# Two tile shapes on TensorE: v beside q and k in 32x32 tiles, router logits straight onto token partitions

## The chip, the core and the metric

The kernel runs on one core of a Trainium2 chip. A core has five engines that work at the same time and wait for each other by semaphores: TensorE (PE, matrix products, with its weight loads shown apart as PEld), VectorE (DVE), ScalarE (ACT), GpSimd (POOL) and SyncE (SP, which here only issues DMAs). The metric is the device time of one launch in microseconds (us).

## What is computed

The input is x, eight images of 64 channels and 96x96 pixels, in float32. A block of two halves is computed, and cut to what matters it is this:

```python
x = x + conv_ref(ln_c(x))             # LN over channels; windowed attention twice (shift 0 and 2)
t = to_tokens(x)
t = t + ffn(ln_t(t))                  # LN over channels; 8 experts, the best 2 of a token
# attention, on each half of the channels (c = 32): 8 heads of 4 channels, windows of 4x4 pixels
q, k, v = split(einsum('oi,bihw->bohw', qkv_w, xh), 3)
lepe = depthwise_conv3x3(v)
attn = softmax(einsum('nhqc,nhkc->nhqk', q * scale, k) + bias)
out  = einsum('nhqk,nhkc->nhqc', attn, v) + lepe
# ffn, on each token
probs = softmax(x @ router_w + router_b)          # 8 logits
top_p, top_i = top_k(probs, 2); top_p = top_p / sum(top_p)
out = sum over the 2 of top_p * (x @ expert_w[e] + expert_b[e])
```

## The kernel before

The images are cut into 192 strips of four pixel rows (384 pixels), a strip into three units of eight windows; two strips make a tile of the second half (96 tiles). The 128 partitions hold four groups of 32 channels: two halves of the channels, plain and rolled.

One function, `pipeline`, runs the same `slot` on every engine. A slot is one unit further along; `LAG` says how many slots after a unit's start each stage works on it, so in one slot each engine does pieces of many stages, in the order in which its `slot` is written. A tile is six slots. 72 slots (12 tiles, one image) are written out before a loop, 72 are the body of a loop of six turns, the rest stands behind it, so PE's program is a long list without repeats inside a turn. No scheduler moves anything: the order on each engine is that of the code. SP and POOL issue their DMAs in that order too, and a wait holds up all that is behind it on the same engine.

PE's stages per tile, with the line that issues them: 6 `score` (L622, 32 products each in 32x32 tiles), 6 `product` (L707, 32 each, 128x32 tiles: contraction over 128 partitions, 32 output partitions), 2 row sums of the softmax (L713, `ones`, four 128x32 tiles), 2 `value` (L647, v, one 128x128 tile), 2 `query_key` (L660 q and L661 k, four 32x32 tiles each), 3 pieces of `conv` (L687, 128x64), 4 `experts` (L607, 128x64), `centre` (L721), `variance` (L638), `tile_sum` (L727) and `tile_variance` (L732), each one 128x128 tile; `router` (L738, logits with the experts on 16 partitions), `logits` (L671, three transposes that put tokens on the partitions), `turn_gates` (L630, a transpose) and `expert_bias` (L746, three products). All is float32; in the trace every float32 product of PE is two weight loads and two matmul records, and a transpose is one of each.

The eight PSUM banks are `bank_s` (two, scores), `bank_o` (bank 2, attention output), `bank_d` (bank 3, row sums), `bank_p` (banks 4 and 5, shared by q, k, v, the two norms, the router and the gates), `bank_c` (6, conv) and `bank_f` (7, experts). ACT takes most things out of PSUM: v (L792), q twice (L810), k (L819), the logits with their bias (L842), and it puts the bias of the next scores into `bank_s` (L802). DVE takes the transposed logits (L989) and works out the gates. POOL spreads k and v into `kx` and `vx` by 8 and 16 DMAs a strip.

## Time and profile before

| | |
|---|---|
| median of three runs | 3484.97 us (3475.89 to 3493.27) |
| the profiled execution, its own time | 3467.97 us |
| its span, first to last instruction | 3466.1 us |
| busy: PE | 3080.1 us (89%) |
| busy: POOL | 2501.0 us (72%) |
| busy: DVE | 2229.3 us (64%) |
| busy: ACT | 1620.3 us (47%) |
| mean granted TensorE clock | 0.943 of full speed |

PE's matmuls are pipelined, and the trace models their ends: a record lasts longer than PE needs before it can go on. What a group costs is therefore read from the start of the group to the start of the next one, not from its length. Where a row of the trace ends in square brackets, the engine was idle before it for that many us, and the name behind the arrow is what ended the idle time; `issue` means that nothing was waited for that the profile shows.

### The profile page before, as it was taken

To read this page: it belongs to the slowest core of one execution; us is meant where nothing else is said; L and a number is where in the kernel's file an instruction comes from. 1 tells how busy PE (TensorE), PEld (TensorE's weight loads), DVE (VectorE), ACT (ScalarE), POOL (GpSimd) and SP (SyncE) were. 2 spreads that over 40 slices of the span, in tenths; PEclk is the share of its full clock that TensorE was granted. 3 is DMA by queue.
4 is the path that set the end of the run, shared out by engine and by line. 5 is a ranking of instruction groups with operands and counts; after the bars stand their busy time and mean duration, and the time that the engine had idled before them with its cause. 6 is when DMAs were issued, how large, how long until landed. Compare 5 with 4: busy or idle time off the path is not lost.

```text
span 3466.1 us, 202400 instructions
## 1 busy us (share of the span) xinstructions
PE 3080.1 (89%) x84772; PEld 1797.6 (52%) x84772; DVE 2229.3 (64%) x4807; ACT 1620.3 (47%) x3362; POOL 2501.0 (72%) x4998
## 2 busy tenths in 40 slices
PE   4899998989989898988889989989889999999996
PEld 2555555555555455554555545555455555555552
DVE  2566666666666666676666667666666666666675
ACT  2554444444444454444445444444444445454541
POOL 4887767767777677777767777777677777777760
PEclk7999999999999899999999999999999999999997
DMA  2456565555656565565556555555555565656555
GB/s 63 109 136 168 145 160 140 160 145 149 160 140 165 140 160 147 146 160 139 159 150 156 153 153 154 155 149 149 149 149 158 150 162 152 168 152 165 156 147 156
DMA packets 447180, 517.72 MB, mean 149 GB/s; under 512 B 120976, under 2 KB 415376, under 8 KB 446096
## 3 DMA queue, kind: packets, MB, share of 16 engines
q1 hardware_dynamic: 280336, 390.69, 41.4%
q0 software_dynamic: 165888, 113.57, 13.2%
q8 instruction: 688, 11.27, 1.4%
q14 instruction: 268, 2.20, 0.2%
HBM read 312.67 MB, written 77.86 MB: 113 GB/s over the span
## 4 chain that ended last, share of the span: by engine, by line
PE 64%; SPq 10%; issue 9%; DMA 9%; DVE 4%; ACT 4%; DVEq 0%; ACTq 0%
PE bank L622 15%; PE bank L707 11%; PE bank L687 10%; PE bank L607 7%; DMA z<-fin 3%; SPq L501 3%; PE bank L713 3%; PE bank L647 3%; PE bank L727 3%; PE bank L660 3%; SPq L531 3%; DMA gate_rows<-gateT 2%; PE bank L721 2%; PE bank L732 2%; PE bank L746 2%
## 5 line engine op out<-in xcount | busy, mean ns | idle before, releaser
L575 POOL DMA_DIRECT2D vx<-vt x3072 | 1555.6, 515 | 458.1 <-PE bank L713 446.1
L563 POOL DMA_DIRECT2D kx<-k_sb x1536 | 737.1, 488 | 419.0 <-issue 268.7
L707 PEld LDWEIGHTS bank<-probT,vx 128*32 128x32 f32 x36864 | 607.9, 150 | 438.2 <-issue 393.9
L622 PE MATMUL bank<-kx,qx 32*32 32x64 f32 x36864 | 705.3, 226 | 107.3 <-issue 79.9
L622 PEld LDWEIGHTS bank<-kx,qx 32*32 32x32 f32 x36864 | 597.5, 111 | 387.8 <-issue 374.2
L707 PE MATMUL bank<-probT,vx 128*32 128x16 f32 x36864 | 672.2, 210 | 139.7 <-issue 126.8
L939 DVE TENSOR_TENSOR gx<-gate_wide,yn_pair 128x768 f32<-128x768 f32 x384 | 365.6, 953 | 463.3 <-DMA gate_wide<-gate_rows 293.6
L796 ACT ACTIVATE prob<-prob 128x512 f32<-128x512 f32 x576 | 360.3, 626 | 267.1 <-DVE prob L951 253.4
L687 PE MATMUL bank<-halo,conv_w 128*64 128x380 f32 (+6 forms) x2592 | 460.3, 482 | 1.1 <-issue 1.1
L951 DVE TENSOR_TENSOR prob<-bank,row_max 128x512 f32<-128x512 f32 x576 | 398.5, 692 | 16.7
L946 DVE TENSOR_REDUCE row_max<-bank 128x32 f32<-128x512 f32 x576 | 382.7, 664 | 38.1 <-PE bank L622 30.0
L1008 DVE STREAM_TRANSPOSE probT<-prob 128x512 f32<-128x512 f32 x576 | 405.2, 704 | 0.2 <-issue 0.2
L607 PE MATMUL bank<-gx,table 128*64 128x384 f32 x1536 | 348.9, 531 | 30.4 <-DVE gx L939 22.3
L966 DVE TENSOR_TENSOR fin<-bank,row_inv 128x384 f32<-128x384 f32 x192 | 106.2, 553 | 368.7 <-ACT row_inv L773 361.0
L802 ACT ACTIVATE bank<-bias_tile 128x512 f32<-128x512 f32 x576 | 339.6, 590 | 0.0
L687 PEld LDWEIGHTS bank<-halo,conv_w 128*64 128x64 f32 x2592 | 176.3, 145 | 236.3 <-issue 225.8
L810 ACT ACTIVATE qx<-bank,table 128x384 f32<-128x384 f32 x384 | 200.4, 572 | 151.4 <-PE bank L660 151.3
L585 POOL DMA_DIRECT2D yn_pair<-yn x384 | 201.2, 532 | 63.6 <-DVE gx L939 39.7
L836 ACT ACTIVATE yrstd<-bank,table 128x384 f32<-128x384 f32 x96 | 55.7, 580 | 351.3 <-PE bank L732 351.3
L792 ACT ACTIVATE v_sb<-bank 128x384 f32<-128x384 f32 x192 | 94.3, 491 | 230.7 <-PE bank L647 230.6
L660 PE MATMUL bank<-xs,table 32*32 32x384 f32 x1536 | 182.5, 513 | 10.3 <-issue 8.8
L647 PE MATMUL bank<-xs,table 128*128 128x384 f32 x384 | 170.6, 527 | 21.9 <-DMA xs<-xn 21.9
(72 smaller groups left out, 2969.7 us busy)
## 6 DMA issues: line engine op xcount, KB each, us to landing
gate_wide<-gate_rows SPq DMA_DIRECT2D x768, 192.0 KB
vx<-vt POOLq DMA_DIRECT2D x3072, 12.0 KB
halo<-xn SPq DMA_DIRECT2D x160, 240.0 KB
kx<-k_sb POOLq DMA_DIRECT2D x1536, 24.0 KB
z<-fin SPq DMA_DIRECT2D x192, 192.0 KB, 5.7
yn_pair<-yn POOLq DMA_DIRECT2D x384, 96.0 KB
xa<-in_x SPq DMA_DIRECT2D x192, 96.0 KB, 4.3
xn<-xa SPq DMA_DIRECT2D x192, 96.0 KB
```

The source lines that it names most:

```text
L563: pool.dma_start(kx[to + m:to + C:4, r % 2, m, :], k_sb[at + m:at + C:4, r % 2, :])\
L575: pool.dma_start(vx[to:to + TOK, r % 2, col:col + 13:4, odd, :], vt[at:at + TOK, r % 2, x::2, :, :].rearrange("p h n k -> p h (n k)"))\
L607: last = MM(bank_f[half * C:(half + 1) * C, 0:SPX], const("experts")[:, p * C:(p + 1) * C], gx[:, p % 2, half, :], start=False, stop=(p == ...
L622: last = MM(bank_s[r % 2][at, w * KEYS:(w + 1) * KEYS], qx[at, kr % 2, win, :, :].rearrange("p a i -> p (a i)"), kx[at, kr % 2, :, win * T ...
L687: last = MM(by_rows(bank_c[half * C:(half + 1) * C, 0:SPX])[:, top:end, low:high], conv_w[:, which, group * 3 + side, :], by_rows(halo[:, ...
L707: last = MM(bank_o[32 * c:32 * c + 32, at * TOK:(at + 1) * TOK], vx[:, kr % 2, :, at % 2, at // 2 * 4 + ba], probT[:, kr % 2, at, ba * TOK ...
L796: S.activation(prob[:, r % 4, :], prob[:, r % 4, :], ACT.Exp).then_inc(exp_made, 1)
L802: S.activation(bank_s[r % 2][:, :], bias_tile[:, :, :].rearrange("p n k -> p (n k)"), ACT.Copy).then_inc(bias_placed, 1)
L939: V.tensor_tensor(gx[:, p % 2, :, :], gate_wide[:, p, :, :], yn_pair[:, r % 2, :, :], ALU.mult)\
L946: V.tensor_reduce(row_max[:, r % 2, :], per_row(bank_s[r % 2][:, :]), AX.X, ALU.max).then_inc(max_made, 1)
L951: V.tensor_tensor(per_row(prob[:, r % 4, :]), per_row(bank_s[r % 2][:, :]), over_keys(row_max[:, r % 2, :]), ALU.subtract).then_inc(shifte ...
L1008: V.transpose(probT[:, kr % 2, j * UW:(j + 1) * UW, :].rearrange("p n k -> p (n k)"), prob[:, r % 4, :]).then_inc(probT_made, 1)
```

## The change

All of PE's work is put into two tile shapes, 32x32 and 128x32. Products with 64 or 128 output partitions are cut into two or four 128x32 tiles of 32 output partitions each: `conv`, `experts`, the four norm products and `expert_bias` (the helper `columns` does four). The contraction of `expert_bias` is widened from 48 to 128 partitions, so `gateT` gets 128 partitions, which POOL clears once. v is no longer projected by a product of its own (`value` is gone): four 32x32 products stand beside those of q and k, and write into `bank_d`. ACT copies v behind k in the same stage. The router swaps its operands: the tokens of `yn` are the stationary side, the router weights move, so the logits come out with the tokens on the partitions; the transposes (`logits`), `logitT` and its ACT copy fall away, and DVE adds the router bias as it takes the logits, at the start of its slot 42 rather than in slot 44. `turn_gates` is a product with the identity in two tiles rather than a transpose. `query_key` stands directly behind `score`. POOL's, SP's and DVE's other work is the same.

```diff
-    centre=0, variance=1, store_xn=2, load_strips=9, value=11, query_key=12,
+    centre=0, variance=1, store_xn=2, load_strips=9, query_key=12,
...
+        def columns(bank, cols, weights, moving, **flags):
+
+            for c in range(0, 128, 32):
+                last = MM(bank[c:c + 32, cols], weights[:, c:c + 32], moving, **flags)
+            return last
...
                     for half in range(2):
-                        last = MM(bank_f[half * C:(half + 1) * C, 0:SPX], const("experts")[:, p * C:(p + 1) * C], gx[:, p % 2, half, :],
-                                  start=False, stop=(p == PAIRS - 1), skip_group_check=True)
+                        for c in range(0, C, 32):
+                            last = MM(bank_f[half * C + c:half * C + c + 32, 0:SPX],
+                                      const("experts")[:, p * C + c:p * C + c + 32], gx[:, p % 2, half, :],
+                                      start=False, stop=(p == PAIRS - 1), skip_group_check=True)
...
-                if st := s.strip("value"):
-                    k, r = st
-                    pe.wait_ge(xs_loaded[r // 2 % 2], (k // 4 + 1) * (XS_DMAS * 16))
...
-                    MM(bank_p[0][:, 0:SPX], wv, xs[:, r % 4, :], start=True, stop=True).then_inc(v_made, 1)
                 if st := s.strip("query_key"):
                     k, r = st
                     if (s.n - LAG["router"] - 1) % TSLOT == 0 and (ti := Slot(s.n - 1, s.turn).tile("router")):
-                        pe.wait_ge(logitT_saved, ti[0] + 1)
-                    if (s.n - LAG["logits"] - 1) % TSLOT == 0 and (ti := Slot(s.n - 1, s.turn).tile("logits")):
+                        pe.wait_ge(fln_made, ti[0] + 1)
                         pe.wait_ge(logit_saved, ti[0] + 1)
+                    if s.later(r, 4):
+                        pe.wait_ge(log_made, k - 3)
                     if r % 2:
 
+                        pe.wait_ge(sq_made, tiles_to(s, (k - 1) // 2 + 3))
                         pe.wait_ge(ln_made, tiles_to(s, (k - 1) // 2 + 3))
-                    wait_alone(pe, v_copied, k + 1)
+                    wait_alone(pe, xs_loaded[r // 2 % 2], (k // 4 + 1) * (XS_DMAS * 16))
                     for g in range(4):
...
                         q_last = MM(bank_p[0][at, 0:SPX], wq[at, at], xs[at, r % 4, :], start=True, stop=True)
-                        k_last = MM(bank_p[1][to, 0:SPX], wk[at, at], xs[at, r % 4, :], start=True, stop=True)
+                        k_last = MM(bank_p[1][to_k, 0:SPX], wk[at, at], xs[at, r % 4, :], start=True, stop=True)
+                        v_last = MM(bank_d[to_v, 0:SPX], wv[at, at], xs[at, r % 4, :], start=True, stop=True)
...
-                            last = MM(by_rows(bank_c[half * C:(half + 1) * C, 0:SPX])[:, top:end, low:high],
-                                      conv_w[:, which, group * 3 + side, :],
...
+                            for c in range(0, C, 32):
+                                last = MM(by_rows(bank_c[half * C + c:half * C + c + 32, 0:SPX])[:, top:end, low:high],
+                                          conv_w[:, which, group * 3 + side, c:c + 32],
...
                     if j == UNITS - 1:
+                        pe.wait_ge(v_copied, strips_to(s, k + 4))
...
-                    MM(bank_p[1][0:GE, 0:SPX], const("router"), yn[:, r % 2, :], start=True, stop=True)\
-                        .then_inc(logitT_made, 1)
+                    for blk in range(TBLK):
+                        for c in range(4):
+                            last = MM(bank_p[1][32 * c:32 * c + 32, blk * GE:(blk + 1) * GE],
+                                      yn[:, r % 2, blk * 128 + 32 * c:blk * 128 + 32 * c + 32], const("router"),
+                                      start=True, stop=True)
+                    last.then_inc(logit_made, 1)
...
+                if ti := s.tile("take_logits"):
+                    k, r = ti
+                    dve.wait_ge(logit_made, k + 1)
+                    V.tensor_tensor(logits[:, :], bank_p[1][:, 0:TBLK * GE], const("router_bias"), ALU.add)\
+                        .then_inc(logit_saved, 1)
```

PE, in the written-out part before the loop, the slot that had `value` and `logits`, up to the next score, before (the lines are those of the list above; the number behind a bank is the bank, the sizes are those of the output):

```order
L713 MATMUL bank3<-probT,table 32x384 x4
L622 MATMUL bank0<-kx,qx 32x64 x32
L607 MATMUL bank7<-gx,table 64x384 x2
L647 MATMUL bank4<-xs,table 128x384
L671 MATMUL bank5<-table,logitT 128x16 x3
L707 MATMUL bank2<-probT,vx 32x16 x32
```

The same place and the slot behind it after the change, where L714 is the row sum, L633 the score, L617 the experts, and L652 to L654 are q, k and v (the first of four such triples is shown):

```order
L714 MATMUL bank3<-probT,table 32x384 x4
L633 MATMUL bank0<-kx,qx 32x64 x32
L617 MATMUL bank7<-gx,table 32x384 x4
L707 MATMUL bank2<-probT,vx 32x16 x32
L633 MATMUL bank1<-kx,qx 32x64 x32
L652 MATMUL bank4<-xs,table 32x384
L653 MATMUL bank5<-xs,table 32x384
L654 MATMUL bank3<-xs,table 32x384
```

v and the transposes have left the slot, v has gone to the next one as a third 32x32 product into bank 3, and the two expert products have become four.

PE again, the slots with `tile_variance`, `expert_bias`, `turn_gates` and `router`, before:

```order
L732 MATMUL bank4<-ysq,table 128x384
L746 MATMUL bank7<-gateT,table 128x128 x3
L622 MATMUL bank1<-kx,qx 32x64 x32
L630 MATMUL bank5<-table,gate_tmp 48x128
L647 MATMUL bank4<-xs,table 128x384
L687 MATMUL bank6<-halo,conv_w 64x4x95 x4
L707 MATMUL bank2<-probT,vx 32x16 x32
L738 MATMUL bank5<-yn,table 16x384
```

And after, where L388 is the helper `columns`, L662 the turn of the gates and L741 the router:

```order
L388 MATMUL bank4<-ysq,table 32x384 x4
L388 MATMUL bank7<-gateT,table 32x128 x12
L633 MATMUL bank1<-kx,qx 32x64 x32
L662 MATMUL bank5<-table,gate_tmp 32x128
L662 MATMUL bank5<-table,gate_tmp 16x128
L687 MATMUL bank6<-halo,conv_w 32x4x95 x8
L707 MATMUL bank2<-probT,vx 32x16 x32
L741 MATMUL bank5<-table,yn 32x16 x12
```

The groups stand in the same places; one product has become two, four or twelve.

## Rows read from the trace of the kernel before

**Rows 1.** The page's first part: busy time, share of the span, instructions.
```profile
span 3466.1 us, 202400 instructions
PE 3080.1 (89%) x84772; PEld 1797.6 (52%) x84772; DVE 2229.3 (64%) x4807; ACT 1620.3 (47%) x3362; POOL 2501.0 (72%) x4998
```

**Rows 2.** The waits of PE: engine line, what ended them, us in total, times, longest.
```profile
PE bank L707 <- issue: 126.8, 117, 2.6
PE bank L622 <- issue: 79.9, 70, 4.4
PE bank L727 <- ACT k_sb L819: 40.4, 51, 1.8
PE bank L622 <- ACT bank L802: 22.7, 56, 2.3
```

**Rows 3.** Timeline of PE in one tile: start us, length us, line, records.
```profile
1707.22 1.11 PE L707 MATMUL bank<-probT,vx 128*32 128x16 f32 x64
1708.16 0.84 PE L713 MATMUL bank<-probT,table 128*32 128x384 f32 x8
1708.93 0.91 PE L732 MATMUL bank<-ysq,table 128*128 128x384 f32 x2
...
1711.79 0.82 PE L647 MATMUL bank<-xs,table 128*128 128x384 f32 x2
1712.54 1.50 PE L687 MATMUL bank<-halo,conv_w 128*64 128x380 f32 x8
1713.97 1.11 PE L707 MATMUL bank<-probT,vx 128*32 128x16 f32 x64
1714.91 0.81 PE L738 MATMUL bank<-yn,table 128*16 128x384 f32 x2
1715.65 1.10 PE L622 MATMUL bank<-kx,qx 32*32 32x64 f32 x64
1716.67 0.87 PE L607 MATMUL bank<-gx,table 128*64 128x384 f32 x4
1717.47 0.51 PE L660 MATMUL bank<-xs,table 32*32 32x384 f32 x1
...
1718.27 1.50 PE L687 MATMUL bank<-halo,conv_w 128*64 128x380 f32 x8
1719.70 1.12 PE L707 MATMUL bank<-probT,vx 128*32 128x16 f32 x64
1720.75 0.91 PE L721 MATMUL bank<-xa,table 128*128 128x384 f32 x2
...
1731.64 0.35 PE L671 MATMUL bank<-table,logitT 16*128 16x16 f32 x3
```

**Rows 4.** Busy time (and records) by stretch; behind POOL: granted clock, DMA share, GB/s.
```profile
118.50:3257.53 3139.03, 2846.51 (x79360) 1668.80 (x79360) 2061.41 (x4443) 1513.50 (x3142) 2335.16 (x4677) 0.95 0.57 152
1736.88:1740.77 3.89, 3.04 (x125) 2.23 (x125) 3.34 (x12) 2.78 (x8) 0.59 (x2) 1.00 0.52 136
```

**Rows 5.** Timeline of PE: restarts after idle time that nothing in the profile ended.
```profile
79.79 0.30 PE L707 MATMUL bank<-probT,vx 128*32 128x16 f32 x7 [1.25 <-issue]
...
84.05 0.25 PE L707 MATMUL bank<-probT,vx 128*32 128x16 f32 x5 [1.99 <-issue]
...
1736.88 1.11 PE L707 MATMUL bank<-probT,vx 128*32 128x16 f32 x63 [1.37 <-issue]
...
1740.77 0.30 PE L622 MATMUL bank<-kx,qx 32*32 32x64 f32 x4 [0.42 <-issue]
...
3320.77 0.86 PE L607 MATMUL bank<-gx,table 128*64 128x384 f32 x3 [0.20 <-issue]
...
3326.07 0.64 PE L622 MATMUL bank<-kx,qx 32*32 32x64 f32 x28 [0.48 <-issue]
```

**Rows 6.** The DMA view of the stretch 118.5 to 3257.53: packets, MB, share of 16 engines.
```profile
q8 instruction: 645, 10.57, 1.5%
```

**Rows 7.** Busy time by stretch, the columns of rows 4, here at half the clock.
```profile
1773.87:1777.28 3.41, 3.41 (x66) 2.19 (x66) 0.93 (x4) 1.62 (x5) 1.36 (x3) 0.50 0.34 113
```

**Rows 8.** Timeline of PE, at half the full clock.
```profile
1773.87 1.65 PE L727 MATMUL bank<-y,table 128*128 128x384 f32 x2 [0.50 <-ACT k_sb L819]
1775.45 0.86 PE L622 MATMUL bank<-kx,qx 32*32 32x64 f32 x23
```

More of the change, by code:

```diff
@@ L317, in metaformer_block @@
         gate_vec = sb("gate_vec", [128, 6, TBLK * 2])
-        gateT = sb("gateT", [TBLK * GE, 2, 128])
+        gateT = sb("gateT", [128, 2, 128])
         gate_wide = sb("gate_wide", [128, PAIRS, 2, SPX])
@@ L629, in slot @@
                     wait_alone(pe, gates_made, k + 1)
-                    nc.tensor.transpose(bank_p[1][0:TBLK * GE, 0:128], gate_tmp[:, 4, :], const("ident"))\
-                        .then_inc(gateT_made, 1)
+                    for c in range(0, TBLK * GE, 32):
+                        last = MM(bank_p[1][c:min(c + 32, TBLK * GE), 0:128], gate_tmp[:, 4, c:min(c + 32, TBLK * GE)],
+                                  const("ident"), start=True, stop=True)
+                    last.then_inc(gateT_made, 1)
                 expert(0)
@@ L664, in slot @@
-                expert(1)
-                if ti := s.tile("logits"):
-                    k, r = ti
-                    pe.wait_ge(ln_made, tiles_to(s, k + (LAG["logits"] - LAG["variance"]) // TSLOT + 1))
-                    wait_alone(pe, logitT_saved, k + 1)
-                    for blk in range(TBLK):
-                        last = nc.tensor.transpose(bank_p[1][:, blk * GE:(blk + 1) * GE],
-                                                   logitT[:, blk * 128:(blk + 1) * 128], const("ident", GE)[:, 0:GE])
-                    last.then_inc(logit_made, 1)
+                    columns(bank_p[1], slice(0, SPX), const("mean"), sq[:, r % 2, :], start=True, stop=True).then_inc(var_made, 1)
@@ L686, in slot @@
                             at = half * SP + skip
[L687 to L690 removed]
+                            for c in range(0, C, 32):
+                                last = MM(by_rows(bank_c[half * C + c:half * C + c + 32, 0:SPX])[:, top:end, low:high],
+                                          conv_w[:, which, group * 3 + side, c:c + 32],
+                                          by_rows(halo[:, r % 2, :])[:, at + top:at + end, low + dw:high + dw],
+                                          start=first[half], stop=(side == 2 and group == 1), skip_group_check=True)
                             first[half] = False
@@ L720, in slot @@
                         pe.wait_ge(q_saved, (2 * k - 3) * 2)
-                    MM(bank_p[0][:, 0:SPX], const("centre"), xa[:, r % 2, :], start=True, stop=True).then_inc(xc_made, 1)
+                    columns(bank_p[0], slice(0, SPX), const("centre"), xa[:, r % 2, :], start=True, stop=True).then_inc(xc_made, 1)
                 if ti := s.tile("tile_sum"):
@@ L726, in slot @@
                     pe.wait_ge(k_saved, strips_to(s, 2 * k + 10))
-                    MM(bank_p[1][:, 0:SPX], const("centre"), y[:, r % 4, :], start=True, stop=True).then_inc(fc_made, 1)
+                    columns(bank_p[1], slice(0, SPX), const("centre"), y[:, r % 4, :], start=True, stop=True).then_inc(fc_made, 1)
                 if ti := s.tile("tile_variance"):
@@ L731, in slot @@
                     pe.wait_ge(q_saved, strips_to(s, 2 * k + 10) * 2)
-                    MM(bank_p[0][:, 0:SPX], const("mean"), ysq[:, :], start=True, stop=True).then_inc(fvar_made, 1)
+                    columns(bank_p[0], slice(0, SPX), const("mean"), ysq[:, :], start=True, stop=True).then_inc(fvar_made, 1)
                 if ti := s.tile("router"):
```

79 lines of the change are left out of this document (34 added, 45 removed).

## The prediction, on record before the changed kernel ran

> **What bounds the kernel now.** I read the busy times first [rows 1]. PE is busy 89% of the span, POOL 72%, DVE 64%, ACT 47%: PE sets the pace. The list of waits says what its idle time ends on [rows 2]. Waits for other engines are small (40 us for k, 23 us for the bias); the largest item is `issue`, 127 us in front of L707 and 80 in front of L622: PE idle, nothing awaited that the profile shows. The third view is the timeline of one tile at full clock [rows 3], read from start to start. There are two kinds of group. Long streams of 384 columns cost about 0.64 us and something for entering and leaving; `score` and `product` are 64 records of little data that go out one behind the other, 0.94 us for the product, 14.7 ns a record with its weight load. Summing such distances over the groups of a tile gives 29.84 us of work. A tile takes longer: the steady stretch from 118.5 to 3257.5 holds 90 tiles (from one `centre` to that of 90 tiles later), 3139.03 / 90 = 34.88 us [rows 4].
>
> What the 5 us between them are is seen at the restarts of `issue` [rows 5]. They lie 256 instructions of PE apart or a multiple of it: from 1736.88 to 1740.77 the trace has 125 matmuls and 125 loads [rows 4] and a few instructions of the sequencer. The queue called instruction brings 645 packets in the stretch, 10.57 MB, so 16 KB each [rows 6]; the 79,360 matmuls and as many loads in it, with some 46 waits and register instructions a tile by the program, make 163,000 instructions, 253 to a packet. So PE's program comes in packets of 256 instructions, and PE stops at a packet's edge when the next is not there. How long a packet takes when PE waits for it is read where one stalled restart follows another 256 instructions later: 4.26 us from 79.79 to 84.05, 3.89 from 1736.88, 5.30 from 3320.77 to 3326.07 [rows 5]; these are the first, one between and the last of 36 such pairs, mean 4.70, median 4.60, shortest 3.59. Per packet PE has 34.88 x 90 / 645 = 4.87 us, and 4.16 us of that is work. **PE is bound by work in some packets and by fetching in others, about evenly.**
>
> **The change, part by part**, per tile, at full clock.
>
> *v.* Two products go: L647 to L687, 0.75 us, and a second of the same kind, together 1.6 us. Added are four 32x32 products in each `query_key`. Today's eight of them take 0.80 us from 1717.47 to 1718.27 [rows 3], q and k of one row group streaming together. Whether a third streams along is not shown for 32x32 tiles: 0 if it does, 0.64 us each if it queues. I take 0, since the four column tiles of L713 stream together (0.77 us for what one 128x128 tile does in 0.84).
>
> *Shape changes.* L707 followed by L713, the same shape, takes 0.94 us; followed by L721, another shape, 1.05 [rows 3]. A change of shape costs 0.11 us. A tile has 29 of them today and 12 after (into and out of 32x32 once a slot): 1.8 us less.
>
> *Cut products.* Experts, norms, conv and bias stream as many columns as before, in column tiles side by side; L607 takes 0.80 and L713, with twice the records, 0.77, so 0 to a small gain: the second weight load no longer shows.
>
> *Router.* L738 (0.74 us) and three transposes (0.35) [rows 3] become 24 records of 16 columns, 24 x 14.7 ns = 0.35, at most 0.74 if it costs what it did. ACT loses a copy and DVE's copy becomes an addition; neither sets the pace.
>
> Group by group: scores 5.95, q, k, v 1.54, products 5.66, conv 3.88, experts, norms and row sums 10 x 0.665, bias 0.64, router 0.38, gates 0.24, leaving 128x32 0.63: **25.57 us, 4.27 us or 14% less work.**
>
> *Waits.* `query_key` now waits for DVE to have taken the logits and for the logarithm of the row sums, before it may write banks 5 and 3; the gates, experts, conv and product are queued behind it on PE. DVE takes the logits first in its slot, and a score of 1.03 us stands between. If that is no cover: some 0.3 us a tile. ACT copies v behind k, so `tile_sum`, which waits for k, sees nothing new, and the next bias comes up to 0.49 us later in two slots of six; it has been waited for 23 us in all. The clearing of `gateT` lies beside the loading of the tables. I take 0 for these; the fetch wait below covers them.
>
> *Instructions.* This is the part that the change adds. Products per tile: v 2 to 8, conv 13.5 to 27, experts 8 to 16, norms 4 to 16, bias 3 to 12, router 1 to 12, less three transposes, one turn becomes two: 57.5 more. At four instructions each, with the transposes' two taken off and the turn's added, 238 instructions, 0.93 of a packet: **7.17 packets a tile become 8.10.** Work per packet falls from 4.16 to 25.57 / 8.10 = 3.16 us, less than the shortest of the 36 waits. So nearly every packet will end on its fetch, and the tile takes 8.10 times what a packet takes to come.
>
> What that is decides. From above: 4.70, the mean of the pairs, which leans long, since only pairs that ended in visible idle time are in it. From below: 3.59, the shortest. Between: today's 4.87 is the mean of the longer of work and fetch. With work at 4.16 and both scattering by 0.8 to 1.0 us, the longer lies about 0.5 above the larger mean, so fetching takes about 4.25. With work now 1.1 below it, the longer is about 4.25 + 0.13. To that comes the clock. It is at 0.95 over the steady stretch [rows 4]; from 1773.87 to 1777.28, behind idle time, it is at 0.50, that is 1.2 GHz [rows 7], and L727 takes 1.58 us start to start, where such a group takes 0.84 at 2.4 GHz [rows 3, 8]. PE will now stop in most packets for about a microsecond, so I expect it there more often, and add 0.1. **4.48 us a packet, 8.10 x 4.48 = 36.3 us a tile, 1.4 more than today's 34.88.** Over 96 tiles: +136 us.
>
> The Trainium skill speaks against this, in "Runtime: NRT & Kernel Launch", section "Instruction fetch mechanics": the sequencer fetches the next 16 KiB page while it executes the current one, and crossing a boundary is "mostly hidden". By that rule the added instructions would cost nothing, and the tile would gain the 4.27 us of work instead of losing 1.4. The packets of 16 KB agree with the page; that they are hidden does not, by the 1.37 us of idle time at 1736.88 [rows 5]. What the time would be by it is the first rival.
>
> **Rivals.** (1) *Fetching keeps ahead.* Then the work counts alone: 34.88 - 4.27 = 30.6 us a tile, 3468 - 410 = 3058 us; POOL, busy 2501 us [rows 1], would not yet stop it. For it: most packet edges show no idle row. It is what the page of the Trainium skill named above would have. Against it: the restarts lie on packet edges and on no other grid. (2) *Fetching is the bound, but quicker.* At 4.31 us a packet the tile is as long as today; this is the point from which the sign turns. At 4.1 it is 33.2 us and 3468 - 161 = 3307. For it: 12 of the 36 pairs lie between 3.89 and 4.14. Against it: 24 do not, and 0.13 for the packets whose work is long comes on top. (3) *The clock.* If half of the packets run at 1.2 GHz, their work of 3.16 us becomes some 5.2 (streams double, the product stays), 0.8 us more than 4.38: 4.78 on the mean, 38.7 us a tile, +368, 3836 us. For it: idle time in most packets. Against it: a slower PE waits less for its fetches. (4) *The shapes do not do what they say*: if the third 32x32 product queued, 1.3 us of work more, in packets that wait anyway: below 0.3 us, inside the range.
>
> **How the numbers follow.** The sum is made against the profiled execution, 3467.97 us, 17 below the median of the runs, 3484.97. 3468 + 136 = 3604; in terms of the median 3621. I give 3610. Chances: the forecast (4.33 to 4.7 us a packet, 3484 to 3772 us) 0.62; as today, 4.29 to 4.33, 0.08; rival 2 0.14; rival 1 0.07; rival 3 0.09. The range goes from 4.2 us a packet (34.0, -83 us: 3385) to 4.7 (38.1, +306: 3774), rounded to 3390 and 3760; rival 1, part of rival 2 and most of rival 3 stay outside. Faster by over 0.5% is rivals 1 and 2, 0.21; within 0.5%, about what can be told from no change, 0.08; slower 0.71.
>
> **What would show it.** The instruction queue brings about 8.1 packets a tile rather than 7.17; the 128x32 and 32x32 groups take 0.67 us where they follow their own shape; the busy time of PE falls while the span does not; `issue` becomes PE's main wait by far, at places that move through the whole tile, 4.2 to 4.7 us apart; the granted clock is below 0.943. Idle time of PE that ends on DVE or ACT, or packets closer than 4.2 us on the mean, would show it wrong.

## The result and the profile after

The changed kernel takes 3641.64 us (3628.97 to 3651.74) against 3484.39 of the kernel before on the same chip: a ratio of 1.0449, 95% interval 1.0406 to 1.0492, so 157 us slower. The profiled execution took 3628.97 us at a mean granted TensorE clock of 0.896 (before 0.943).

The page's first part of the changed kernel, to be read beside [rows 1]: busy time, share of the span, instructions.

```profile
span 3627.1 us, 224906 instructions
PE 2902.4 (80%) x96196; PEld 1817.5 (50%) x96196; DVE 2229.2 (61%) x4807; ACT 1548.7 (43%) x3266; POOL 2500.9 (69%) x4999
```

PE is busy 178 us less and the span is 161 us longer, with 11,424 more matmul records. No other engine has become busier; PE's weight loads have, by 20 us. So PE is idle 339 us more, and its list of waits says for what (columns as in [rows 2]: engine, line, what ended the wait, us in total, times, longest):

```profile
PE bank L707 <- issue: 227.2, 219, 2.6
PE bank L633 <- issue: 191.7, 112, 5.4
PE bank L652 <- issue: 38.4, 35, 2.3
PE bank L707 <- DVE fin L973: 36.2, 32, 1.4
PE bank L388 <- ACT k_sb L820: 32.9, 58, 2.1
...
PE bank L633 <- ACT bank L803: 25.4, 32, 5.3
```

`issue` in front of product and score was 207 us; it is 419 now, and it has come up before q too (L652, 38 us; 9 before). Added up over all lines, `issue` ends 549 us of PE's idle time where it was 227: 322 of the 339 us. One wait for another engine is new in size: 36 us of the product for DVE's `fin`, where [rows 2] has no such line.

One stretch of the timeline of PE in the changed kernel, for the cost of the groups (start, length, line, records, as in [rows 3]):

```profile
1713.85 1.05 PE L707 MATMUL bank<-probT,vx 128*32 128x16 f32 x64
1714.74 0.83 PE L714 MATMUL bank<-probT,table 128*32 128x384 f32 x8
1715.39 0.82 PE L388 MATMUL bank<-ysq,table 128*32 128x384 f32 x8
1716.04 0.83 PE L388 MATMUL bank<-gateT,table 128*32 128x128 f32 x24
1716.80 1.10 PE L633 MATMUL bank<-kx,qx 32*32 32x64 f32 x64
```

From start to start the product takes 0.89 us (0.94 before), the row sum 0.65 (0.77), the norm product 0.65 in four tiles (0.84 in one). Into the other shape, from the bias to the score, it is 0.76. The work did get shorter, as the diff says.

The restarts of PE in the changed kernel that end on `issue` and lie one packet apart, and two such stretches as windows (columns of [rows 4]):

```profile
1731.03 0.88 PE L633 MATMUL bank<-kx,qx 32*32 32x64 f32 x49 [1.65 <-issue]
...
1735.50 0.35 PE L707 MATMUL bank<-probT,vx 128*32 128x16 f32 x10 [0.76 <-issue]
...
1744.68 0.53 PE L707 MATMUL bank<-probT,vx 128*32 128x16 f32 x23 [1.38 <-issue]
...
1748.61 0.30 PE L633 MATMUL bank<-kx,qx 32*32 32x64 f32 x4 [1.20 <-issue]
```

```profile
1731.03:1735.50 4.47, 3.71 (x127) 2.38 (x126) 2.74 (x5) 2.06 (x4) 0.45 (x1) 1.00 0.61 183
1744.68:1748.61 3.93, 2.73 (x125) 1.94 (x125) 3.60 (x13) 3.21 (x8) 1.66 (x5) 1.00 0.31 102
```

They hold 253 and 250 records and a few instructions of the sequencer, some 256 in all, as [rows 4, 5] had it before; they last 4.47 and 3.93 us, and each ends on idle time. There are 165 such pairs in the trace (36 before), mean 4.52 us.

That these stops are waits for packets is seen when the ends of the instruction queue's transfers are laid beside PE's restarts. Of 445 stops of the changed kernel that end on `issue` and last over 0.15 us, 83% end between 1.2 and 1.7 us after a packet has landed (87% of 211 in the kernel before). Of PE's restarts after other waits 3% do, and of its matmuls taken at even distances 10%.

What a tile costs is read from 90 tiles, from the third `centre` to the 93rd. The window of the changed kernel, and its line of the DMA view:

```profile
57.93:3329.90 3271.97, 2661.78 (x89538) 1680.43 (x89540) 2041.05 (x4386) 1442.04 (x3040) 2329.47 (x4666) 0.90 0.55 144
```

```profile
q8 instruction: 723, 11.85, 1.6%
```

3271.97 / 90 = 36.36 us a tile, 723 / 90 = 8.03 packets a tile, 4.53 us a packet. The same 90 tiles of the kernel before:

```profile
64.13:3188.92 3124.79, 2826.86 (x79176) 1661.99 (x79176) 2041.04 (x4384) 1506.90 (x3126) 2329.05 (x4665) 0.95 0.57 151
...
q8 instruction: 643, 10.53, 1.5%
```

That is 34.72 us, 7.14 packets, 4.86 us a packet. The chain of waits (shares of the span, SPq is SP's queue) of the kernel before, then of the changed one:

```profile
PE 64%; SPq 10%; issue 9%; DMA 9%; DVE 4%; ACT 4%; DVEq 0%; ACTq 0%
...
PE 73%; issue 17%; ACT 4%; DVE 3%; DMA 2%; SPq 2%; DVEq 0%; ACTq 0%
```

The share of PE and of `issue` went up; the kernel before has another 19% on SP's queue and the transfers, which will matter below.

### The profile page after: what moved, and what is told of

Same layout as the page of the kernel before. It is cut to its first block, busy times and chain, and to the rows that moved or that the text cites. A ratio compares the mean times of both kernels' runs of the same rounds, so it can differ in the third digit from the quotient of the medians.

```text
span 3627.1 us, 224906 instructions
## 1 busy us (share of the span) xinstructions
PE 2902.4 (80%) x96196; PEld 1817.5 (50%) x96196; DVE 2229.2 (61%) x4807; ACT 1548.7 (43%) x3266; POOL 2500.9 (69%) x4999
## 4 chain that ended last, share of the span: by engine, by line
PE 73%; issue 17%; ACT 4%; DVE 3%; DMA 2%; SPq 2%; DVEq 0%; ACTq 0%
PE bank L633 18%; PE bank L707 13%; PE bank L687 11%; PE bank L388 10%; PE bank L617 8%; PE bank L652 4%; PE bank L714 3%; PE bank L653 2%; ACT qx L811 1%; PE bank L654 1%; ACT bank L803 1%; ACT k_sb L820 1%; PE bank L741 1%; SPq L508 1%; PE bank L662 1%
## 5 line engine op out<-in xcount | busy, mean ns | idle before, releaser
L707 PEld LDWEIGHTS bank<-probT,vx 128*32 128x32 f32 x36864 | 677.0, 150 | 558.6 <-issue 508.3
L633 PE MATMUL bank<-kx,qx 32*32 32x64 f32 x36864 | 741.3, 230 | 218.3 <-issue 191.7
L707 PE MATMUL bank<-probT,vx 128*32 128x16 f32 x36864 | 696.7, 209 | 265.7 <-issue 227.2
L633 PEld LDWEIGHTS bank<-kx,qx 32*32 32x32 f32 x36864 | 623.3, 114 | 480.4 <-issue 474.7
L687 PE MATMUL bank<-halo,conv_w 128*32 128x380 f32 (+6 forms) x5184 | 507.6, 499 | 6.2 <-issue 6.1
L617 PE MATMUL bank<-gx,table 128*32 128x384 f32 x3072 | 370.1, 550 | 33.4 <-DVE gx L941 18.0
L652 PE MATMUL bank<-xs,table 32*32 32x384 f32 x1536 | 252.7, 610 | 64.7 <-issue 38.4
L687 PEld LDWEIGHTS bank<-halo,conv_w 128*32 128x32 f32 x5184 | 206.1, 121 | 193.0 <-issue 169.4
L654 PE MATMUL bank<-xs,table 32*32 32x384 f32 x1536 | 271.8, 613 | 29.0 <-issue 29.0
L653 PE MATMUL bank<-xs,table 32*32 32x384 f32 x1536 | 264.9, 613 | 31.8 <-issue 31.8
```

Source lines behind the costliest of these rows:

```text
L617: last = MM(bank_f[half * C + c:half * C + c + 32, 0:SPX], const("experts")[:, p * C + c:p * C + c + 32], gx[:, p % 2, half, :], start=Fal ...
L633: last = MM(bank_s[r % 2][at, w * KEYS:(w + 1) * KEYS], qx[at, kr % 2, win, :, :].rearrange("p a i -> p (a i)"), kx[at, kr % 2, :, win * T ...
L652: q_last = MM(bank_p[0][at, 0:SPX], wq[at, at], xs[at, r % 4, :], start=True, stop=True)
L687: last = MM(by_rows(bank_c[half * C + c:half * C + c + 32, 0:SPX])[:, top:end, low:high], conv_w[:, which, group * 3 + side, c:c + 32], by ...
L707: last = MM(bank_o[32 * c:32 * c + 32, at * TOK:(at + 1) * TOK], vx[:, kr % 2, :, at % 2, at // 2 * 4 + ba], probT[:, kr % 2, at, ba * TOK ...
```

## The experiments

All are read the same way, from the same 90 tiles of each trace. The ratio is to the kernel before on the same chip.

| kernel | median us | ratio [95%] | tile us | packets a tile | us a packet | clock there |
|---|---|---|---|---|---|---|
| before | 3484.39 | 1 | 34.72 | 7.14 | 4.86 | 0.95 |
| changed | 3641.64 | 1.0449 [1.0406, 1.0492] | 36.36 | 8.03 | 4.53 | 0.90 |
| e1_cuts_alone | 3551.67 | 1.0227 [1.0184, 1.0270] | 35.42 | 7.79 | 4.55 | 0.94 |
| e2_v_router | 3506.50 | 1.0097 [1.0068, 1.0126] | 35.07 | 7.23 | 4.85 | 0.92 |
| e3_pad | 3803.38 | 1.0930 [1.0874, 1.0986] | 38.53 | 8.07 | 4.78 | 0.92 |
| e4_balance | 3419.49 | 0.9849 [0.9804, 0.9893] | 34.18 | 7.14 | 4.78 | 0.97 |
| e5_after_balance | 3597.47 | 1.0333 [1.0298, 1.0367] | 35.94 | 8.03 | 4.47 | 0.92 |
| e6_v_router_balance | 3452.69 | 0.9916 [0.9886, 0.9945] | 34.59 | 7.23 | 4.78 | 0.95 |
| e7_less_dma | 3471.65 | 0.9953 [0.9927, 0.9978] | 34.92 | 8.03 | 4.35 | 0.93 |
| e8_bf16_product | 3393.17 | 0.9748 [0.9731, 0.9765] | 33.96 | 5.57 | 6.10 | 0.88 |
| e9_balance_experts | 3398.35 | 0.9757 [0.9738, 0.9777] | 34.12 | 7.14 | 4.78 | 0.96 |
| e10_best | 3348.28 | 0.9589 [0.9550, 0.9629] | 33.53 | 5.58 | 6.01 | 0.89 |
| e11_bf16_less_dma | 3099.14 | 0.8907 [0.8871, 0.8944] | 30.91 | 5.58 | 5.54 | 0.96 |
| e12_after_bf16 | 3385.39 | 0.9731 [0.9694, 0.9769] | 33.94 | 6.48 | 5.24 | 0.84 |

The theory: PE's time is that of its program's packets, and the change adds packets. The main rival: the packets are fetched ahead, and the loss is something else that the change brought (its waits, its shapes, the clock).

**The cutting alone**, on the kernel before (experts, norms, conv and bias, v and router as they were):

```diff
-                    MM(bank_p[1][:, 0:SPX], const("mean"), sq[:, r % 2, :], start=True, stop=True).then_inc(var_made, 1)
+                    columns(bank_p[1], slice(0, SPX), const("mean"), sq[:, r % 2, :], start=True, stop=True).then_inc(var_made, 1)
...
-                            last = MM(by_rows(bank_c[half * C:(half + 1) * C, 0:SPX])[:, top:end, low:high],
...
+                            for c in range(0, C, 32):
+                                last = MM(by_rows(bank_c[half * C + c:half * C + c + 32, 0:SPX])[:, top:end, low:high],
```

> The kernel before, with the cutting into 128x32 tiles alone (experts, norms, conv, expert bias); v, the router and the transposes stay as they were. PE's program grows by 170 instructions a tile, from 7.17 packets to 7.84; its work falls from 29.8 us a tile to about 28.0. Theory (PE stops at the edges of packets of 256 instructions until the next is there): 4.66 us a packet, between the 4.87 of before and the 4.51 of after by the work in it, 36.5 us a tile, about 3630 us, 4 to 5% slower than before. Rival (the work of PE sets the time, so what slows the changed kernel is not the cutting): 1.8 us a tile less, about 3300 us.

Measured 3551.67 us, +2.3%: slower, but by half of what the theory's number said. The waits of PE in it:

```profile
PE bank L632 <- issue: 185.5, 141, 4.6
PE bank L718 <- issue: 137.4, 189, 2.7
PE bank L390 <- ACT k_sb L832: 41.0, 62, 1.9
```

The new idle time is `issue` again, 323 us before score (L632) and product (L718) against 207; the wait for k is what it was. The sign speaks for the theory, since no product here streams more columns than before. The size was wrong by the time of a packet: I had put it at 4.66 us, between the kernel before and the changed one by the work in it, and it took 4.55. The packets were near, 7.79 a tile where I had 7.84.

**v and the router alone**: the changed kernel with every cut undone, the router as three 128x128 products.

```diff
-            for c in range(0, 128, 32):
-                last = MM(bank[c:c + 32, cols], weights[:, c:c + 32], moving, **flags)
-            return last
+            return MM(bank[:, cols], weights, moving, **flags)
...
-                        for c in range(4):
-                            last = MM(bank_p[1][32 * c:32 * c + 32, blk * GE:(blk + 1) * GE],
-                                      yn[:, r % 2, blk * 128 + 32 * c:blk * 128 + 32 * c + 32], const("router"),
-                                      start=True, stop=True)
+                        last = MM(bank_p[1][:, blk * GE:(blk + 1) * GE],
+                                  yn[:, r % 2, blk * 128:(blk + 1) * 128], const("router"), start=True, stop=True)
```

> The changed kernel with all the cutting undone: v beside q and k, and the router with the tokens stationary (three 128x128 products a tile), but experts, norms, conv and bias in their old shapes. 7.27 packets a tile (7.17 before), work about 28.1 us a tile. Theory of packets: 4.77 us a packet, 34.7 us a tile, about 3445 us, 0.5 to 1% faster than before. Rival (work sets the time): 1.7 us a tile less, about 3305 us. A rival that the move of v and the logits is what costs: slower than before.

Measured 3506.50 us, 1% slower where I expected up to 1% faster. By its sign this is what the last rival said, that the move of v and the logits costs by itself. The busy time of PE fell, the packets did not:

```profile
58.90:3214.87 3155.97, 2732.09 (x80346) 1702.42 (x80346) 2046.44 (x4384) 1432.15 (x3040) 2329.14 (x4666) 0.92 0.56 149
```

```profile
q8 instruction: 651, 10.67, 1.5%
```

PE's waits in it:

```profile
PE bank L700 <- issue: 186.2, 156, 2.6
PE bank L629 <- issue: 110.8, 82, 4.1
PE bank L700 <- DVE fin L964: 37.0, 30, 3.0
```

651 packets instead of 643, at 4.85 us instead of 4.86. PE is busy 95 us less in the 90 tiles, and idle time took that back: added up over all lines `issue` is 349 us (227 before), and the product's wait for `fin` 37 (5). The tile is 0.35 us longer. 0.09 packets of 4.25 us would be 0.38; the wait for `fin`, 0.33 us a tile more, and the lower clock (0.92) are there too, and how the 0.35 us part among the three I can't say. So the part of the change that lightens PE gained nothing here, with the packets about as many; that it was the packets alone which took the gain back is not shown.

**More packets and nothing else**: ten tiny products (one column) ahead of each `product` in the kernel before, 240 instructions of PE a tile, about what the change adds. Their results are not used.

```diff
+                    for c in range(10):
+                        MM(bank_o[32 * (c % 4):32 * (c % 4) + 32, 500:501], const("ident")[:, 0:32], const("ident")[:, 0:1],
+                           start=True, stop=True)
```

> The kernel before with ten small products of one column in front of every unit's attention products, into a column that nothing reads: 240 instructions a tile more, as many as the changed kernel adds, with no change of shapes and nothing moved. Each small product is two records of 14.7 ns, so 1.8 us of work a tile more. Theory of packets: 8.12 packets a tile at 4.77 us, 38.7 us a tile, about 3840 us. Rival (instructions cost their work alone): 1.8 us a tile more, about 3640 us.

Measured 3803.38 us, +9.3%, near the theory's 3840 and far from the 3640 of the added work alone. The page of this kernel, its busy line and the line of the instruction queue, then PE's waits:

```profile
PE 3303.5 (86%) x96292; PEld 1961.0 (51%) x96292; DVE 2234.4 (58%) x4807; ACT 1615.1 (42%) x3362; POOL 2501.2 (65%) x4998
...
q8 instruction: 776, 12.71, 1.5%
```

```profile
PE bank L622 <- issue: 286.7, 191, 5.8
PE bank L710 <- issue: 116.2, 124, 2.4
```

It has the packets of the changed kernel (776 in the whole run, both) and the shapes, order and waits of the kernel before. PE is busy 223 us more, and the span is 365 us longer in the profiled executions; `issue`, added up over all lines, is 429 us, 202 more than in the kernel before. This is the run that decides between the theory and the rival: packets cost time by themselves. The added work is 120 records a tile of 14.7 ns [rows 3], 1.76 us or 169 us in 96 tiles, and the run is 328 us longer than the kernel before on the same chip (3475.04 us). By the Trainium skill, "Runtime: NRT & Kernel Launch", section "Instruction fetch mechanics", crossing a 16 KiB boundary is mostly hidden. This run does not agree with that.

**Levelling the packets**: conv's pieces are put into other slots, so that packets with much work and packets with little lie less apart. The instructions are the same. On the kernel before (e4), on the changed one (e5), and on the version with v and router alone (e6):

```diff
-    store_z=24, load_halo=29, load_tile=33, conv=34, y_first=37, y_second=38, y_third=38, tile_sum=39, tile_variance=40, router=41, logits=44,
+    store_z=24, load_halo=29, load_tile=33, conv=32, y_first=36, y_second=38, y_third=38, tile_sum=39, tile_variance=40, router=41, logits=44,
...
+CONV_AT = {0: 0, 1: 1, 3: 2}
...
-                if (ti := s.in_tile("conv")) and ti[2] < len(SIDES):
+                if (ti := s.in_tile("conv")) and ti[2] in CONV_AT:
+                    side = CONV_AT[side]
```

> The kernel before with the three pieces of the conv in other slots: the two with the least work of PE get one each (the third stays where the second stood), and the first addition after it a slot earlier. The same instructions, the same work; only the work of a packet varies less, since a packet is about as long as a slot. Theory of packets (a packet takes the longer of its work and its fetch): 4.68 us a packet rather than 4.87, 33.6 us a tile, about 3340 us. Rival (the sum of work sets the time, and the fetch only shows in a few places): no change, 3468 to 3485 us.

> The changed kernel with the three pieces of the conv moved as in e4. 8.10 packets a tile, 3.2 us of work in each. Theory of packets: nearly every packet ends on its fetch however the work is spread, so little is gained: 4.42 us a packet rather than 4.51, about 3560 us; the gain is smaller than twice that of e4 (56 us there). Rival (the slots left short by v and the logits are what costs the changed kernel): most of the 4.5% comes back, about 3480 us.

> e2 (v beside q and k, router with tokens stationary, nothing cut) with the conv moved as in e4, so that the slots that lost v and the logits get a piece of conv. 7.27 packets a tile, 28 us of work. Theory of packets, with the lesson of e2 that a packet with little work gains nothing: evenly filled packets of 3.85 us take about 4.55 us, 33.1 us a tile, 3300 to 3380 us, faster than both kernels. Rival (v beside q and k costs by itself, by waits between engines or by the clock): no better than e4's 3419 us.

Measured 3419.49, 3597.47 and 3452.69 us. By the ratios the first is 1.5% faster than the kernel before, the second 1.1% faster than the changed one, with the same number of packets in each pair and a shorter time for each (4.78 for 4.86, 4.47 for 4.53). In e4 that is less than half of the gain I expected. A packet's time as the longer of its work and its fetch would give a gain, but the gain is not where that puts it. Added up over all lines `issue` stays: 220 us in e4 against 227 in the kernel before, 570 in e5 against 549 in the changed one. What fell in e4 is PE's busy time (3014 us for 3080), at a clock of 0.97 for 0.95; in e5 it is PE's busy time (2884 for 2902) and the waits for `fin` (2 us for 36) and for k (under 1 us for 33). So these runs don't show that levelling shortens the stops. A new wait came in with e4, and its chain went over to SP's queue and the transfers:

```profile
PE bank L608 <- DVE gx L941: 87.6, 42, 9.4
...
SPq 32%; DMA 32%; PE 23%; issue 10%; DVE 1%; ACT 1%; ACTq 0%; DVEq 0%
```

The kernel before waited 22.3 us for `gx`. And e6 misses as e2 did, and comes out as its rival said, no better than e4: it has less work than e4, its ratio is 0.7% higher, and it has 0.09 packets a tile more. The tile is 0.41 us longer than e4's, as e2's is 0.35 longer than that of the kernel before, though the wait for `fin` is 3 us here. That speaks against this wait as the cause in e2; the packets and the clock (0.95 against 0.97 in e4) remain.

**Less traffic beside the fetch**: the changed kernel writes each gate to 8 of 64 partitions. Most products with a gate are left out of the result by this; PE's instructions are the same.

```diff
-                        sp.dma_start(gate_wide[odd * C:(odd + 1) * C, p, :, :],
-                                     by_expert[odd, p].unsqueeze(0).broadcast_to([C, 2, SPX]))\
+                        sp.dma_start(gate_wide[odd * C:odd * C + 8, p, :, :],
+                                     by_expert[odd, p].unsqueeze(0).broadcast_to([8, 2, SPX]))\
```

> The changed kernel with gate_wide loaded into 8 partitions of 64 rather than all (the rest stays zero, so most of the gates' products are left out of the result; all instructions of the engines stay). About a quarter of the DMA traffic falls away. If the time from a packet's edge to the next packet is queueing behind other DMA packets, it shrinks: at 4.0 us a packet rather than 4.5, about 3270 us. If it is the fetch's own latency, the time stays at 3625 to 3645 us.

Measured 3471.65 us, 4.7% less than the changed kernel, and between the two expectations. The 90 tiles of this kernel:

```profile
62.48:3204.97 3142.49, 2609.80 (x89536) 1661.60 (x89538) 2042.25 (x4388) 1443.18 (x3040) 2338.40 (x4668) 0.93 0.43 113
```

The DMA engines are busy 43% rather than 55%, and a packet takes 4.35 us rather than 4.53, with as many packets. `issue` is still PE's main wait (179 us before the product, 169 before the score). The transfer of a packet ends about 0.2 us sooner after PE has gone over the edge before (the last section has these times). So part of a packet's time is spent behind other transfers, and most of it is not.

**Fewer packets**: attention weights and v in bfloat16 in the kernel before, so that a product needs one load and one matmul instead of two of each. The result is rounded by this.

```diff
-        vx = sb("vx", [128, 2, 32, 2, WIN // 2 * 4])
+        vx = sb("vx", [128, 2, 32, 2, WIN // 2 * 4], BF16)
...
-        probT = sb("probT", [128, 2, WIN, KEYS])
+        prob_b = sb("prob_b", [128, 4, UK], BF16)
+        ones_b = sb("ones_b", [128, CH], BF16)
+        probT = sb("probT", [128, 2, WIN, KEYS], BF16)
...
-                    S.activation(prob[:, r % 4, :], prob[:, r % 4, :], ACT.Exp).then_inc(exp_made, 1)
+                    S.activation(prob_b[:, r % 4, :], prob[:, r % 4, :], ACT.Exp).then_inc(exp_made, 1)
```

> The kernel before with the attention weights and v in bfloat16, so that the products of L707 and the row sums of L713 are one weight load and one matmul each instead of two (rounded to bfloat16 there). PE's program loses 400 instructions a tile: 5.6 packets rather than 7.17. Work falls by about 3.8 us a tile to 26.0, as much as the changed kernel's did (25.6), but with 2.5 packets fewer than that. Theory of packets: 5.6 packets at 5.15 us, 28.8 us a tile, 2890 us, or up to 3000 if POOL, busy 26 us a tile, begins to hold it up. Rival (work alone sets the time): 3100 us. In any case it parts what the changed kernel has in common with it, less work, from what it has not, fewer instructions.

Measured 3393.17 us, 2.5% faster. The packets fell to 5.57 a tile as meant, and the time did not follow: a plain miss of 400 us. The chain of waits of this kernel, then its waits of PE and the first of VectorE:

```profile
SPq 38%; DMA 34%; PE 13%; issue 11%; ACT 2%; DVE 2%; DVEq 0%; ACTq 0%
```

```profile
PE bank L625 <- ACT bank L806: 167.0, 189, 2.3
PE bank L730 <- ACT k_sb L823: 158.6, 90, 3.0
PE bank L610 <- DVE gx L943: 95.3, 45, 8.5
PE bank L625 <- issue: 35.7, 23, 3.4
```

```profile
DVE gx L943 <- DMA gate_wide<-gate_rows: 461.3, 108, 10.7
```

`issue` is nearly gone from PE's list (63 us over all lines, 227 in the kernel before), so the packets are no longer the bound. The chain lies on SP's queue and the transfers for 72%. VectorE stands 461 us before `gx` for the gates (294 in the kernel before), and PE for ACT and VectorE.

**The gates' transfer as the next bound**: e8 with the edit of e7 (most products with a gate left out).

> The kernel before with attention weights and v in bfloat16, and each gate written to 8 of 64 partitions instead of all (24 KB instead of 192 KB for a pair of experts), so that most products with a gate are left out of the result; instructions of every engine stay as in the bfloat16 kernel. Theory: the gates' transfer is what ended PE's gain in that kernel (3393 us where the count of packets promised 2900 to 3000). Then VectorE's 461 us of waits for it go and the time falls to 28 to 31 us for each of some 90 tiles plus 330 us of head and tail: 2850 to 3120. Rival one, that it is the chain of bias, logits, exponent and product inside a unit of attention (PE waits 167 us for ACT's bias, ACT 367 us for VectorE's prob): unchanged, 3330 to 3400. Rival two, that the lighter traffic only quickens the fetch of packets, as it did by 4.7% in the changed kernel: 3230.

Measured 3099.14 us, 294 us below e8, inside the theory's range and far from both rivals. The chain of this kernel:

```profile
PE 67%; ACT 12%; DVE 11%; issue 7%; DMA 2%; SPq 1%; DVEq 1%; POOL 0%; ACTq 0%; POOLq 0%
```

It has gone back from the transfers to PE. What ended e8's gain was therefore the traffic of the gates. Whether by the length of that transfer or by what it delays behind it on SP's queue, these runs don't part.

**The change where packets are few**: the edit of e8 on the changed kernel.

> The changed kernel with attention weights and v in bfloat16: some 400 fewer instructions of PE for each tile, 1674 instead of 2074, which is 6.5 packets of 256. It is to be set against the bfloat16 version of the kernel before (3393 us, 5.6 packets a tile). Theory, that the change costs by the count of packets alone: 6.5 packets at 4.3 to 4.5 us are 28 to 29.4 us, less than the 34 us that a tile takes in that version, which waits for the gates' transfer; so the change costs nothing there: 3350 to 3440, within 1.5% of 3393. Rival, that its cost lies in its own forms (the shorter columns, the third stream, the clock) and comes wherever it is made: the same 4.5% as on the kernel before, 3545.

Measured 3385.39 us, ratio 0.9731 [0.9694, 0.9769]; e8 has 0.9748 [0.9731, 0.9765]. Against e8 the change costs nothing. The chain of this kernel, and the first of its waits of PE:

```profile
SPq 42%; DMA 36%; issue 11%; PE 7%; DVE 2%; ACT 1%; POOL 1%; DVEq 0%; ACTq 0%; POOLq 0%
```

```profile
PE bank L620 <- DVE gx L945: 145.7, 61, 9.5
PE bank L390 <- ACT k_sb L824: 143.7, 91, 2.8
PE bank L710 <- issue: 138.0, 117, 2.4
```

PE still stops for packets (138 us before the product, 81 before the score), but the tile is set by the transfers, and the stops lie beside them. This shows that the cost is there only where PE's program sets the pace. It does not by itself show that it is the count of packets rather than the shapes: 1.6 us a tile of any origin on PE would be hidden here too. For the count speak e3 (packets without the shapes, +9.3%) and the place of the stops in the changed kernel, 1.2 to 1.7 us behind the landing of a packet. The third stream in 32x32 tiles with the shorter router, and few packets more, costs 1% (e2), of which the cause is open.

**Moving the experts as well**: e4 with the two experts' pairs behind conv and behind the product, and the end of the tile a slot later, against e4's wait for `gx`; then the same with e8's edit.

```diff
-                expert(0)
...
-                expert(1)
...
+                expert(0)
                 if u := s.unit("product"):
...
+                expert(1)
```

> e4 with the expert products later in their slot (behind conv, and behind the attention products) and the output a slot later, since in e4 PE waited 88 us for the gated tokens (22 us before). The same packets. Theory: of the 88 us some 60 go, and part of them is taken back as fetch waits: 3370 to 3410 us against 3419 of e4. Rival: DVE, which now waits longer for the experts, holds up the next scores, and it is slower than e4.

Measured 3398.35 us: right, and 2.4% faster than the kernel before, all in float32. The wait for `gx` fell from 87.6 to 15.1 us, and one of the product for DVE's `probT` came up, 78.6 us. The chain lies on SP's queue and the transfers for 63%, as in e4.

> The kernel before with three edits together, each of which ran alone or in a pair: the conv pieces and the experts' products put in other places of the program, and attention weights and v in bfloat16. The two moves alone gave 0.9757, the bfloat16 product alone 0.9748. Theory: in the bfloat16 kernel it is no longer the packets of PE's program that set the time (536 packets of the instruction queue against 688) but the transfer that spreads the gates: VectorE stands 461 us before gx for it (294 us in the kernel before), and of the chain of waits 72% lies on SP's queue and the DMAs. The two moves leave SP's queue as it is, except that the end of a tile comes a slot later, so they give back only what PE waits for gx (95 us): 3270 to 3340. Rival, that PE's program still sets the time and the gains multiply: 0.976 x 0.975 of 3484, some 3310, and less than that if the packets' wait goes altogether (3150). Time alone does not tell these apart; the waits do: by the theory VectorE's wait for the gates' transfer stays above 300 us, and PE's waits end on ACT and DVE, not on the next packet.

Measured 3348.28 us, 0.9589 [0.9550, 0.9629], the fastest of those that compute the whole function (its product is rounded to bfloat16), and just above the theory's range. The waits of VectorE and the first of PE in it:

```profile
DVE y L987 <- DMA z2t<-z: 559.7, 95, 12.9
DVE gx L945 <- DMA gate_wide<-gate_rows: 226.6, 154, 3.4
```

```profile
PE bank L711 <- DVE probT L1014: 373.1, 92, 7.1
PE bank L650 <- DMA xs<-xn: 89.7, 51, 14.2
PE bank L626 <- ACT bank L808: 37.9, 41, 2.3
```

PE's waits end on DVE, on a transfer and on ACT, not on the next packet, and the transfers are the bound (86% of the chain on SP's queue and DMAs). But VectorE's wait for the gates, which I put above 300 us, is 227; it waits 560 us for `z2t` instead. Another transfer of the same queue had come to be the late one.

## Why the prediction was right

Forecast 3610 us, measured 3641.64; range 3390 to 3760; slower at 0.71. By its steps:

*What bounds the kernel.* Right, by e3, by e8 and by the place of the stops: adding packets costs time without any other change, taking them away removes `issue` from PE's waits, and most stops end 1.2 to 1.7 us after a packet has landed. That a packet takes just the longer of its work and its fetch stays an assumption of the sum: e4 and e5 don't show it.

*The work.* Right in direction and near in the pieces that can be read: a 128x32 group behind its own shape takes 0.65 us (0.665 put down), a change of shape 0.11, and the third 32x32 product streams along: the twelve products of q, k and v take 0.84 us, where eight of q and k took 0.80 [rows 3]. The first of the twelve and the product behind them:

```profile
1742.16 0.48 PE L652 MATMUL bank<-xs,table 32*32 32x384 f32 x1
...
1743.00 0.30 PE L707 MATMUL bank<-probT,vx 128*32 128x16 f32 x7
```

The product takes 0.89 instead of 0.94, which I had not seen. The work that was saved came back as idle time: PE is busy 178 us less and idle 339 us more.

*The packets.* 8.10 a tile put down, 8.03 measured; the ratio to before is 1.13 and 1.12.

*The time of a packet.* 4.48 put down, 4.53 measured, but made up otherwise. When the edges of packets are laid between two restarts by counting records, the packets that saw only the full clock take about 4.3 us, where I had 4.38; those that saw half the clock, some three in ten, take 5.0 to 5.2. This is an estimate, since some records are missing and it depends on which packets are counted. By it fetch and overlap came out some 0.05 lower, and the clock cost about 0.2 instead of 0.1: the term of the clock was half of what it is, and the other hid part of it. That the sum came so near to what was measured is luck in part. The granted clock of 0.90 in the 90 tiles against 0.95 is the row for that, and rival 3 had this mechanism with too high a price.

*The sum.* 36.3 us a tile, 36.36 measured. The measured difference is 157 us and mine was 136, though the tile after was right: I set it against 34.88, read over a stretch from one `centre` to another, and the 90 tiles read here give 34.72 for the kernel before; 96 x (36.36 - 34.72) is 157.

*The waits.* I took 0 for the new ones. The bias is waited for 25 us (23 before), k for 33 (40 before): right. The product's wait for `fin` of DVE came up from 5 us to 36. Whether it lies in stops that the packets make anyway or adds up to 0.3 us a tile, no run separates cleanly. Against its adding up speaks e5: there it is gone, and the tile gains 0.42 us by the move of conv, no more than the 0.54 that the same move gives the kernel before, which had no such wait to lose.

*The rivals.* Fetching kept ahead (3058) and quicker fetching (3307) are out by the result, and e7 says how near the second was: with lighter traffic a packet takes 4.35 us, hardly above the 4.31 where the sign would have turned, and that kernel is level with the one before (0.9953). What I had overlooked in both is the next bound. I looked for it in POOL; it is SP's queue and the transfers. The kernels whose chain has gone over to these (e4, e6, e8, e9, e10, e12: 61% to 86% of it) all take 33.5 to 34.6 us a tile, so 30.6 or 33.2 was hardly to be had by a faster PE alone. One of them is the changed kernel itself with fewer packets (e12, 33.94).

## What to carry to other kernels

Where PE works in many small instructions, count the instructions as well as the work: lay the packets of the instruction queue over the tile, and ask of each edit whether it changes their number or only what is in them. Cutting a product into column tiles leaves its columns alone and multiplies its instructions: it cost time here where the program's packets were the bound (e1), and the whole change cost none where the transfers were (e12). One bfloat16 product in place of the float32 one took away 22% of the packets. And after each bound that goes, look at the chain of waits again: here it went over to the transfers at once, and the gain stopped at 2.5%.

## What the runs showed of the hardware

PE's program is brought in packets of 256 instructions, and here each took 4.2 to 4.5 us when PE waited for it. Worked out by laying the packets' transfers beside the instructions, the transfer ends on the mean some 2.8 us after PE has gone over the edge into the packet before, and PE, where it stands, goes on 1.4 us after that end: 4.2 us in all. With lighter traffic (e7) the first part is some 2.6 us; the second is the same.

A product record with its load goes out in 14.7 ns [rows 3], so a packet filled with nothing but these, 128 records and 128 loads, takes 1.9 us of PE, less than half of its fetch. By that such a stretch of this kernel can't run faster than its packets come, however short its products are.

The clock went down roughly as PE stopped more: in the 90 tiles it is 0.97 in e4, 0.95 in the kernel before, 0.90 in the changed one, and 0.84 in e12, which waits for packets and for transfers. It is not in strict order (e8, with few stops for packets, has 0.88), but in each pair where work was taken out of a PE that waits, it fell: 0.95 to 0.92 from the kernel before to e2, 0.97 to 0.95 from e4 to e6. Part of the work that was saved may have been paid back so, at the 1.2 GHz of [rows 7]; no run shows how much.
